# First batch of an attention and ternary FFN kernel: one set of ternary weights earlier, one set of weight scales later, three more constant products

## The reference, cut to what matters

```python
x = L0_attn_x                                   # (8, 512, 256) float32, 8 batches
xn = layernorm(x)                               # without weights
x = x + attn(xn, Wq, Wk, Wv, Wo) + ffn(xn, W_fc, ln_w, ln_b, W_proj)

def attn(xn, ...):                              # 16 heads of 16, a window of 64 keys
    q, k, v = xn @ Wq, xn @ Wk, xn @ Wv
    scores = q . k_window / 4; attn = softmax(scores); ctx = attn . v_window
    return ctx @ Wo

def absmean(W):                                 # ternary weights
    gamma = mean(|W|) + 1e-6
    return sign(W / gamma) * min(round(|W / gamma|), 1)

def ffn(xn, ...):
    h = gelu(xn @ absmean(W_fc).T)              # 256 -> 1024
    h = layernorm(h) * ln_w + ln_b
    return h @ absmean(W_proj).T                # 1024 -> 256
```

## Time and profile before

| | |
|---|---|
| median of 3 runs | 396.02 us (395.78 to 396.27) |
| profiled execution | 395.66 us, of which the profile's span is 393.9 us |
| mean granted TensorE clock | 0.987 of full speed |
| PE busy | 371.4 us, 94% |
| DVE busy | 321.0 us, 81% |
| ACT busy | 287.5 us, 73% |
| POOL busy | 231.7 us, 59% |

### The profile page before, as it was taken

How to read it: one execution, slowest core, us unless ns; L and a number is a source line. 1 busy time by engine, 2 the same in 40 slices (tenths; PEclk the granted TensorE clock), 3 DMA queues, 4 the chain that set the end, 5 groups by cost and what they waited for, 6 DMA issues and landing times.

```text
span 393.9 us, 13464 instructions
## 1 busy us (share of the span) xinstructions
PE 371.4 (94%) x5798; PEld 266.0 (68%) x5798; DVE 321.0 (81%) x649; ACT 287.5 (73%) x329; POOL 231.7 (59%) x186
## 2 busy tenths in 40 slices
PE   1896899999999999999999999999999999999994
PEld 0344655876588776776587766776677775788873
DVE  3798988599969996899959997799959898998554
ACT  2656168978978698767977698767886698768871
POOL 7901025866685547755575448755576548679871
PEclk9899699999999999999999999999999999999999
DMA  8578029501932087022920177022921176003002
GB/s 283 160 91 95 2 47 165 83 3 33 153 37 52 15 151 109 2 65 46 188 28 27 41 149 109 4 63 46 189 27 30 39 107 100 2 17 81 30 20 78
DMA packets 30684, 29.22 MB, mean 74 GB/s; under 512 B 5664, under 2 KB 29280, under 8 KB 30624
## 3 DMA queue, kind: packets, MB, share of 16 engines
q1 hardware_dynamic: 30048, 27.83, 38.7%
q10 hardware_dynamic: 576, 0.52, 1.3%
HBM read 7.35 MB, written 4.19 MB: 29 GB/s over the span
## 4 chain that ended last, share of the span: by engine, by line
PE 85%; DVE 6%; ACT 4%; DMA 1%; POOL 1%; ACTq 1%; issue 1%; POOLq 1%
PE small L1625 15%; PE big L1564 13%; PE small L1636 10%; PE big L1538 9%; PE big L1615 7%; PE big L1550 6%; PE big L1603 5%; PE big L1578 5%; PE small L1652 5%; PE big L1608 4%; PE big L1584 3%; PE big L1526 2%; PE small L1642 2%; DMA x_in<-in_x 1%; DVE negmax L1026 1%; ACT qk_split L731 1%
## 5 line engine op out<-in xcount | busy, mean ns | idle before, releaser
L578 POOL TENSOR_TENSOR p_parts<-probs,p_parts 128x1024 f16<-128x1024 f32 x64 | 136.3, 2134 | 112.6 <-ACT p_parts L762 112.6
L761 ACT ACTIVATE probs<-big,exp_scale 128x1024 f32<-128x1024 f32 x64 | 71.5, 1117 | 22.8 <-PE big L1608 20.7
L1026 DVE TENSOR_REDUCE negmax<-big 128x8 f32<-128x1024 f32 x64 | 77.5, 1222 | 4.8 <-PE big L1584 3.4
L762 ACT ACTIVATE p_parts<-big,exp_scale 128x1024 f16<-128x1024 f32 x64 | 71.4, 1115 | 0.0
L1625 PE MATMUL small<-proj_t,g_hi 128*128 128x256 f16 x256 | 57.7, 273 | 0.0
L1625 PE MATMUL small<-proj_t,g_lo 128*128 128x256 f16 x256 | 57.5, 272 | 0.0
L776 ACT ACTIVATE g_hi<-big,lnw_s 128x512 f16<-128x512 f32 x64 | 39.8, 690 | 16.4 <-PE big L1615 16.4
L1564 PE MATMUL big<-fc_t,xt_hi 128*128 128x512 f16 x128 | 48.5, 379 | 2.2 <-ACT gel L749 1.2
L1564 PE MATMUL big<-fc_t,xt_lo 128*128 128x512 f16 x128 | 48.5, 379 | 0.0
L1020 DVE SCALAR_TENSOR_TENSOR g_lo<-big,lnw_s,g_hi 128x512 f16<-128x512 f32 x64 | 46.5, 745 | 1.7 <-ACT g_hi L776 1.3
L1062 DVE SCALAR_TENSOR_TENSOR y_bufs<-small,rs,res 128x256 f32<-128x256 f32 x32 | 15.5, 483 | 29.9 <-PE small L1625 26.8
(11 more groups left out here) (133 smaller groups left out, 810.0 us busy)
## 6 DMA issues: line engine op xcount, KB each, us to landing
q_stack<-qk_split SPq DMA_DIRECT2D x48, 128.0 KB, 4.3
k_stack<-qk_split SPq DMA_DIRECT2D x44, 128.0 KB, 6.3
x_in<-in_x SPq DMA_DIRECT2D x8, 512.0 KB, 5.7
out<-y_bufs SPq DMA_DIRECT2D x32, 128.0 KB, 2.8
v_odd<-v_even SPq DMA_DIRECT2D x16, 132.0 KB, 2.5
v_odd<-v_even SPq DMA_DIRECT2D x16, 99.0 KB, 2.2
gel<-in_w_fc SPq DMA_DIRECT2D x1, 1024.0 KB, 6.5
y_bufs<-in_w_proj SPq DMA_DIRECT2D x1, 1024.0 KB, 8.3
```

Of the source, the lines that this page charges most:

```text
L578: g.tensor_tensor(p_lo[:, (b * NJ + j) % PB], probs[:, (b * NJ + j) % PB], p_hi[:, (b * NJ + j) % PB], ALU.subtract).then_inc(*sig(p_lo_re ...
L761: s.activation(probs[:, (b * NJ + j) % PB].rearrange("p i (u q) -> p u i q", u=2), st, ACT.Exp, scale=exp_scale[:, 0:1]).then_inc(*sig(exp ...
L762: s.activation(p_hi[:, (b * NJ + j) % PB].rearrange("p i (u q) -> p u i q", u=2), st, ACT.Exp, scale=exp_scale[:, 0:1]).then_inc(*sig(p_hi ...
L1026: v.tensor_reduce(negmax[:, :, j], slot[b, "sa", j][:].rearrange("p a (u k) -> p (a u) k", k=P), AX.X, ALU.max, negate=True).then_inc(*sig ...
```

## The change

Five edits, all in the lists of the first batch. PE: job sums 1 goes directly behind qk 0, and spread 1 moves from ahead of sums 1 to behind fc 1. ACT: `weight_upper(1)` moves from between the two qk_upper to behind gelu 1. DVE: `ternary(0)` goes directly behind thresholds(0), both qk_lower follow, and largest(1), scales(1), thresholds(1) and weight_lower(1) come after them. Warm 1 has eight products, not five. Nothing is computed otherwise than before, and the lists of SP and POOL stay as they are.

```diff
         FIRST = [(0, "wmax", 0), (0, "spread", 0), (0, "warm", 0), (0, "xt", 0), (0, "sums", 0), (0, "wmax", 1),
-                 (0, "warm", 1), (0, "qk", 0), (0, "spread", 1), (0, "sums", 1), (0, "qk", 1), (0, "fc", 0),
-                 (0, "fc", 1), (0, "fc", 2), (0, "fc", 3), (0, "v", 0), (0, "crow", 0), (0, "sa", 0), (0, "sa", 1),
+                 (0, "warm", 1), (0, "qk", 0), (0, "sums", 1), (0, "qk", 1), (0, "fc", 0), (0, "fc", 1), (0, "spread", 1),
+                 (0, "fc", 2), (0, "fc", 3), (0, "v", 0), (0, "crow", 0), (0, "sa", 0), (0, "sa", 1),
...
             absolute(1)
             qk_upper(0, 0)
-            weight_upper(1)
             qk_upper(0, 1)
             load_upper_keys()
             gelu(0, 0)
             gelu(0, 1)
+            weight_upper(1)
             gelu(0, 2)
...
             thresholds(0)
+            ternary(0)
+            qk_lower(0, 0)
+            qk_lower(0, 1)
             largest(1)
-            ternary(0)
             scales(1)
-            qk_lower(0, 0)
             thresholds(1)
             weight_lower(1)
-            qk_lower(0, 1)
             split_norm()
             ternary(1)
...
-            WARM = (3, 5)
+            WARM = (3, 8)
```

## The result

The changed kernel takes 398.04 us (median of 4 executions, 397.63 to 398.16) against 396.08 us before: a ratio of 1.0053, with an interval of 1.0041 to 1.0065. It is slower by 2.0 us. The forecast was 398.8, in a range of 397.2 to 401.0. The profiled execution took 398.0 us, of which 396.2 are the span.

A forecast was written before the change was run, and what follows sets the result against it. DVE was taken to decide before 42.5 us, through proj_t and the maxima. Proj_t 4.15 us later, less 1.42 of slack, made +2.75; on the 396.02 median that gave 398.8, range 397.2 to 401.0.

The forecast's parts named there:

- The one slack: DVE's 1.42 us wait for v_upper: proj_t ending after 32.76 us would delay the maxima and all that follows.
- Eight products: Three more products in warm 1 on PE, costing nothing, shorten the gap before qk 0 from 1.74 to 1.1 us.
- the good bound: Qk 0 on PE at full clock, a gain of 1.7 us; the other bound was a gain of nothing.
- Sums, ACT, DVE: Steps from qk 1's end (21.68) through gelu 0 (26.85) and the wait for w_hi to proj_t at 35.5, 4.15 later.
- the favourable bound: Ternary(0) on DVE gets through before POOL's fill, so fc_t ends about 2 us sooner; set at nothing for the time.
- The path behind it: PE from the first maximum to the end: maxima, batch 1's xt and what follows all 2.75 us later.
- rival B's bad side: Low clock over batch 1's xt lasts longer and slows batch 1's qk 0: 2 to 2.6 us more, 401; chance 0.06.
- the sum: All steps together: +2.75 us on the profiled execution's 395.66, giving 398.4.
- this offset: 0.36 us by which the median of the runs before, 396.02, stood above the profiled execution, 395.66.
- A: Rival: the clock falls before qk 0 on PE all the same, maxima 4.45 us later, 400.5; chance 0.18.
- B's good side: Rival: full clock returns before batch 1's xt, saving 2.0 us, 396.8; chance 0.08.
- C: Rival: PE's head start reaches the end, worth up to 2 us (394.0), if proj_t isn't on the path; chance 0.04.

The follow-up runs named there:

- R5: The changed kernel with weight_upper(1) behind gelu 3 instead of behind gelu 1: 400.09 us, ratio 1.0112 to the kernel before.
- R4: The changed kernel with weight_upper(1) ahead of gelu 0, behind the four DMA issues: 395.16 us, ratio 1.0006 to the kernel before.
- r9: r7 with seven more products in PE's idle time between fc 2 and fc 3: 393.59 us, ratio 0.9945 to the kernel before.
- r1: The changed kernel with five products in warm 1 instead of eight: 398.55 us, ratio 1.0073 to the kernel before.
- r6: The kernel before with ternary(0) ahead of largest(1) on DVE, all else as it was: 397.31 us, ratio 1.0038.
- r7: The changed kernel with spread 1 directly behind qk 1, weight_upper(1) ahead of gelu 0, and DVE's list reordered: 395.69 us, ratio 0.9996 to the kernel before.
- r3: The changed kernel with split_norm and ternary(1) ahead of weight_lower(1) on DVE: 397.18 us, ratio 1.0023 to the kernel before.
- second series: The changed kernel run once more, beside later follow-up kernels on one chip: 397.42 us, ratio 1.0042 to the kernel before.
- R8: The changed kernel with no products in warm 1: 400.41 us, ratio 1.0112 to the kernel before.
- r11: The kernel before, order unchanged, with eight products in warm 1 and 22 more in PE's idle times up to batch 1's xt: 394.23 us, ratio 0.9966.
- r2: The kernel before with only warm 1 changed, from five to eight products: 395.13 us, ratio 0.9989.

## Why the prediction was right

The mechanism, its place and nearly all its times up to the maxima were as forecast; 398.04 lies 0.8 us below the forecast. Part of that closeness is luck, since two errors of 0.4 and 0.5 us had opposite signs (below).

*What bounds.* The one slack was read as 1.42 us, the wait for v_upper. The profile of the changed kernel bears it out: proj_t is 3.86 us later and the maxima 2.34, so 1.52 us were absorbed. R5 shows that beyond the slack delay is paid in full (proj_t 2.74 us later than in the changed kernel, the maxima 2.73). R4 doesn't test it: proj_t came at 31.30 + 2.35 = 33.65, 0.9 beyond the slack, but in an execution where v was later still, and no profile shows its faster group.

*Eight products.* The forecast took the good bound, 1.7 us, and qk 0 ended where it said (18.8). Three profiles with eight products and the early rise of the clock (the two of the changed kernel and r9) have gaps of 1.09, 1.09 and 0.97 us and a fast qk 0; the kernel before, with the same early rise and five products, has 1.74 us and a slow one. That the new gap is short enough is thus shown; that eight are needed is not, since r1 and r6 are fast with five. Gaps of 1.74 us (kernel before), 1.80 (r6) and 2.54 (r4) were followed by a granted clock of 0.50, 1.6 us behind the gap at most, while gaps of 2.02 in r7 and 2.24 in r3 were not. The rule of the page "TensorE: Matmul & The Clock Gate" of the Trainium skill (HAM oscillation), that it is idle gaps a good deal longer than these that lower the clock, is not borne out by the first three. What the step missed is that the products have a price of their own when the clock is late: 3.5 and 3.6 us for the eight in r5 and r4, and qk 0 0.6 to 0.8 us later. It costed them at nothing.

*Sums, ACT, DVE.* Qk 1's end was given as 21.68 and is 21.55, gelu 0 26.85 and 26.72, the second half of w_lo 30.9 and 30.7, proj_t 35.5 and 35.20. The steps agree to 0.1 to 0.3 us, but all on the same side, and that makes the maxima 41.41 and not 41.8: a delay of 2.34 us and not 2.75. For ternary(0) the favourable bound came true, and, as forecast, it gave nothing, since gelu waited for ACT's issues. DVE's wait for w_hi was forecast as about 2 us and is 2.67, because DVE was ready at 26.62 and not at 27.4; the wait ends with w_hi either way, so that cost nothing.

*The path behind it.* The delay was taken to stay constant to the end. In the profile it grew by 0.48 us between xt and g_lo, through the longer stretch at low clock (rival B's bad side, in small), and behind the last y_bufs the profile of the kernel before has 0.49 us more. In the second series, with a shorter stretch, the whole difference is 1.65. So against the 398.4 that the sum gave for the profiled execution the terms are -0.41 for the sum up to the maxima, +0.48 for the clock behind it and -0.49 for the end, and together they make the 398.0 measured. The rest is the 0.36 us that was added because the kernel before had its median above its profiled execution; the changed kernel has its median only 0.04 above. The end and this offset stand in no step of the prediction's argument, and each is about as large as the error of the sum.

*The rivals.* A did not occur in the two profiles of the changed kernel. R8 shows a slow qk 0 with the later work moved by 2.7 us, dearer than the 1.7 taken for it, as all of qk 0 was slow; but there the clock had not risen yet, which is not the fall that A describes. B's good side, 2.0 us, was oversized: with the clock held all the way r11 gains 1.4 by the medians and 1.0 up to the last y_bufs. C is excluded for the change, but r7's three good executions and r9 show that the head start does reach the end once w_hi comes ahead of the gelus.

What stays open: why the clock drops in some executions of the same kernel and not in others; the granted clock of 7 against 5 executions (r4) shows only that it does. That the slower groups of r3 and r7 have the cause seen in r4's profile is inferred from their mean clock and, for r7, from r9; no profile shows them. Open as well is what makes the last stores take 0.5 to 0.7 us longer in three of the profiles.

## What to carry to other kernels

On an engine that works its list in order, moving an instruction moves everything queued behind its wait: before weight scales are put off, look for what stands behind their consumer (here split_norm and ternary(1) behind weight_lower(1)) and how much slack the next common point has. A head start on an engine that isn't the bound is worth nothing until the later queueing is mended too. Idle gaps of 1.5 to 2.5 us on PE ahead of important work can cost more than themselves, through the clock, though not every such gap did here; products into a free PSUM buffer, no more than fit the gap, took 1.4 us off the median of the kernel before. And before a difference of half a microsecond is explained, compare the same late instruction in both profiles: here up to 0.7 us of such differences lay behind the last computation.

## What the runs showed of the hardware that was not expected

- The same work runs at different levels of the TensorE clock at the same place from one execution to the next. The transpose behind batch 0's xt (L1658, near 13 us), ahead of which all these kernels have the same work, takes 0.27 us in four of the fourteen profiles and 0.37 in ten; the eight products behind it take from 1.89 to 3.62 us. R4's executions differ by 2.7 us (394.9 to 397.6), with mean granted clocks of 0.991 and 0.987.
- The granted clock in the profile leaves out the time before the first rise: it gives 1.00 in r8 from 16 to 21 us, where matmuls that take 0.38 us at full clock take 0.63. There the durations have to be read, and a mean of 0.987 or 0.991 doesn't count that stretch.
- The spread of the times can shrink to a fifth with no change in the mean clock: 1.2 us for the kernel before and 0.23 us for r2 beside it, which adds three products and has 0.991 in all executions, as most of the others have. R11, with all gaps filled, has 0.23 us too, and the kernel before beside it 0.78. Which part of this is the clock isn't shown.
- From the end of the last y_bufs to the end of the span it takes 2.2 us in ten profiles and 2.3 to 2.95 in four, whatever the order of work.
- A DVE instruction of 3x3 elements was held for 2.12 us beside a POOL memset of 2.02 us (r2), and the memset for 2.98 us when DVE's tensor_scalar came first (the changed kernel). Of the two long instructions the first to start had the way: before, the memset (16.58) ahead of the tensor_scalar (16.62), in the changed kernel the tensor_scalar (16.35) ahead of the memset (16.61). The page "SBUF — State Buffer" of the Trainium skill (SBUF: two separate sides) says so of the pair of ports that these two engines share, and the trace agrees in these two cases. The 3x3 instruction fits less plainly: in the profile it starts at 16.48, 0.08 us before the memset, and yet is held to its end; an earlier, shorter memset ran until 16.50, and whether that one held it first isn't shown. In the changed kernel a scalar_tensor_tensor (fc_t, 2.35 us) was not slowed by the memset of 2.98 us, which ran on beside it from 17.6 to 19.6.
